# An attention and FFN kernel on Trainium2: narrower waits on the last x1 stores, a gate product two tiles later, two clears on another engine

## What is computed

```python
W = weights[condition]                                  # a style matrix (32x32) per sequence
h = einsum('bct,bcd->bdt', x, W)
q, k, v = split(clip(h @ w_qkv.T, -8, 8))
q, k = layer_norm(q), layer_norm(k)                     # with weight and bias
probs = softmax(causal(q @ k.T * scale + alibi))        # 32 heads of 16
x1 = x + (probs @ v) @ w_out.T

y = einsum('bsi,boi->bso', x1, weight[adapter_ids])     # one of 8 adapters (512x512) per sequence
logits = y @ gate_w
r = sum(top_k(logits, 2))                               # the sum of the two largest
shared = relu(y @ up_w)**2 @ down_w
routed = ((y @ fc1_w @ expert_w) * r) @ fc2_w
out = x1 + layer_norm(shared + routed)
```

## Time and profile before

| what | us |
|---|---|
| median of 3 executions | 1146.95 |
| lowest and highest of them | 1144.14, 1147.49 |
| the profiled execution | 1143.86 |
| its span, from first to last instruction | 1142.1 |

### The profile page before, as it was taken

The page is one execution under the profiler, slowest core; times in us unless marked ns, Lnnn a source line. Parts: engine busy times, 40 slices in busy tenths (PEclk is TensorE's granted clock), DMA queues, the critical chain, the costliest instruction groups (busy, mean ns, idle before and its releaser), DMA issues.

```text
span 1142.1 us, 27399 instructions
## 1 busy us (share of the span) xinstructions
PE 1095.8 (96%) x10996; PEld 892.1 (78%) x10996; DVE 682.4 (60%) x1042; ACT 603.0 (53%) x985; POOL 710.2 (62%) x610
## 2 busy tenths in 40 slices
PE   5999999999999999999999699999999999999994
PEld 3778888888888888888877578787878888787883
DVE  5767666666667666666665156565656545554432
ACT  4466767777767677777776233425161524333220
POOL 4366888888888887888766255556455454533342
PEclk9999999999999999999999899999999999999997
DMA  7035555555555556565487724232514223030100
GB/s 273 30 87 179 182 185 183 184 181 189 177 185 180 186 181 208 184 182 190 150 285 269 292 86 127 92 93 75 133 56 120 70 83 102 28 84 28 46 28 37
DMA packets 95277, 160.77 MB, mean 141 GB/s; under 512 B 46385, under 2 KB 47153, under 8 KB 89777
## 3 DMA queue, kind: packets, MB, share of 16 engines
q1 hardware_dynamic: 77504, 114.23, 30.8%
q0 software_dynamic: 12224, 34.10, 9.4%
q10 hardware_dynamic: 5424, 10.71, 2.6%
HBM read 93.97 MB, written 42.47 MB: 119 GB/s over the span
## 4 chain that ended last, share of the span: by engine, by line
PE 91%; DMA 3%; DVE 2%; issue 1%; SPq 1%; ACT 0%; POOL 0%; DVEq 0%; ACTq 0%; POOLq 0%
PE bank L628 22%; PE pair L812 16%; PE bank L788 15%; PE bank L718 10%; PE bank L805 8%; PE bank L668 7%; PE pair L645 3%; PE pair L690 2%; PE bank L676 2%; PE bank L618 2%; PE bank L703 1%; DMA x_rows<-x1t 1%; PE bank L656 1%; PE bank L758 1%; DMA vx<-v_hl 1%
## 5 line engine op out<-in xcount | busy, mean ns | idle before, releaser
L1664 POOL TENSOR_TENSOR w_lo<-w2t,w_hi 128x2048 fp32r<-128x2048 f32 x38 | 175.1, 4608 | 35.8 <-ACT w_hi L972 32.1
L628 PE MATMUL bank<-wqkv_hi,h_hi 128*128 128x512 f32 x384 | 153.6, 400 | 0.1
L1726 POOL TENSOR_TENSOR u_lo<-act,u_hi 128x512 fp32r<-128x512 f32 x64 | 82.7, 1293 | 113.2 <-ACT u_hi L1165 113.0
L628 PE MATMUL bank<-wqkv_hi,h_lo 128*128 128x512 f32 x384 | 149.8, 390 | 0.0
L628 PE MATMUL bank<-wqkv_lo,h_hi 128*128 128x512 f32 x384 | 149.6, 390 | 0.0
L1513 DVE TENSOR_TENSOR act<-act 128x512 f32<-128x512 f32 x59 | 67.0, 1135 | 57.1 <-ACT act L1161 57.1
L812 PE MATMUL pair<-down_hi,u_hi 128*128 128x512 f32 x256 | 100.9, 394 | 0.0
L812 PE MATMUL pair<-down_hi,u_lo 128*128 128x512 f32 x256 | 100.8, 394 | 0.0
L788 PE MATMUL bank<-yT_hi,up_hi 128*128 128x512 f32 x256 | 100.7, 394 | 0.0
L812 PE MATMUL pair<-down_lo,u_hi 128*128 128x512 f32 x256 | 100.3, 392 | 0.0
L788 PE MATMUL bank<-yT_hi,up_lo 128*128 128x512 f32 x256 | 99.8, 390 | 0.0
(11 more groups left out here) (178 smaller groups left out, 2919.2 us busy)
## 6 DMA issues: line engine op xcount, KB each, us to landing
w2t<-in_w SPq DMA_DIRECT2D x38, 1024.0 KB
vx<-v_hl SPq DMA_DIRECT2D x128, 68.0 KB
x_rows<-x1t SPq DMA_DIRECT2D x32, 256.0 KB, 3.7
x1g<-x_rows SPq DMA_DIRECT2D x32, 256.0 KB, 2.9
kx<-k_hl SPq DMA_DIRECT2D x124, 64.0 KB
ffn_high<-w_high SPq DMA_DIRECT2D x20, 256.0 KB, 3.7
ffn_low<-w_low SPq DMA_DIRECT2D x20, 256.0 KB, 3.4
stage<-in_wqkv SPq DMA_DIRECT2D x3, 1024.0 KB, 8.0
```

Of the source, the lines that this page charges most:

```text
L628: m = e.matmul(into, a[:, c, :], b[:, n, c, :], start=(c == 0 and k == 0), stop=(c == KC - 1 and k == 2))
L1664: e.tensor_tensor(w2_lo[:, :, :], w2t[:, :, :], w2_hi[:, :, :].bitcast(F32), ALU.subtract).then_inc(d_wlo, 1)
L1726: e.tensor_tensor(u_lo[n % FC][:, :], act[n % 2][:, :], u_hi[n % FC][:, :].bitcast(F32), ALU.subtract) \
```

## The change

- **x1 stores.** On ScalarE the wait for both a_store semaphores at u chunk 5 becomes a wait for a_store[0] at chunk 6 and one for a_store[1] at chunk 7.
- **y of group 1.** On SP both halves (1 MB each) are loaded after the load of adapter 27 instead of ahead of the store of x1 tile 31. The gate product of group 1 goes from behind the up chunks of group 0 to behind the down products of its second tile, its transposes and gate_weights(1) to the third tile; the groups after it stay as they are.
- **Adapter 26.** SP loads it after the store of x1 tile 28, no longer ahead of the vx copies of tile 29. The low part of down is fetched in two pieces, seven chunks ahead of w2_hi of slot 26 and one after o_hi of tile 31.
- **Start.** The clears of kx and vx go to GpSimd, as 32-bit words, the first behind the third style product, the second behind v's low part of tile 0. The low half of wo on DVE goes behind v of tile 0. DVE waits for the adapter ids alone, and copies the style ids seven steps later, behind a semaphore of their own.

The diff, cut to its core:

```diff
@@ SP
             for dst, src in ((ids_row[:, :], adapter_ids.broadcast_to([P, BATCHES])),
-                             (ids_col[:, :], adapter_ids.rearrange("o b -> b o")),
-                             (style_col[:, :], style_ids.rearrange("o b -> b o"))):
+                             (ids_col[:, :], adapter_ids.rearrange("o b -> b o"))):
                 e.dma_start(dst, src).then_inc(s_ids, 16)
+            e.dma_start(style_col[:, :], style_ids.rearrange("o b -> b o")).then_inc(s_style, 16)
...
             spread_k(T - 2)
-            load_w2(slot_up(0))
...
             store_x1(T - 4)
+            load_w2(slot_up(0))
             spread_v(T - 1)
...
             store_x1(T - 2)
-            upto(e, "r", T - 1)
-            load_back(1, 0, 0, KC)
-            load_back(1, 1, 0, KC)
             store_x1(T - 1)
...
                 if slot_down(m) < SLOTS:
                     load_w2(slot_down(m))
+                if m == 0:
+                    upto(e, "r", T - 1)
+                    load_back(1, 0, 0, KC)
+                    load_back(1, 1, 0, KC)
@@ TensorE
-                    e.wait_ge(m_down, 32)
+                    e.wait_ge(m_down, 48)
...
-                if ahead:
+                if ahead and m:
                     gate_products(m + 1)
...
                     down(m, t)
-                    if ahead and t == 0:
+                    if m == 0 and t == 1:
+                        gate_products(1)
+                    if ahead and t == (0 if m else 2):
                         turn_gates(m + 1)
@@ ScalarE
             fetch(m_route, route_lo[:, :, :], 1, UP_CHUNKS, ROUTE_CHUNKS)
+            upto(e, "o", T - 1)
+            upto(e, "x1", T - 2)
+            fetch(m_down, down_lo[:, 0:FC - 1, :], 1, UP_CHUNKS + ROUTE_CHUNKS, FC - 1)
             high_w2(slot_up(0))
...
-            upto(e, "x1", T - 2)
-            fetch(m_down, down_lo[:, :, :], 1, UP_CHUNKS + ROUTE_CHUNKS, FC)
+            upto(e, "ot", T - 1)
+            fetch(m_down, down_lo[:, FC - 1:FC, :], 1, CHUNKS - 1, 1)
...
                     if n == EARLY:
                         upto(e, "x1", T - 1)
-                        for k in range(2):
-                            e.wait_ge(a_store[k], 16 * (T // 2))
+                    elif EARLY < n < FC:
+                        e.wait_ge(a_store[n - EARLY - 1], 16 * (T // 2))
...
-                if ahead:
+                if ahead and m:
                     gates_out(m + 1)
...
+                    if m == 0 and t == 1:
+                        gates_out(1)
@@ DVE
-            e.wait_ge(s_ids, 48)
+            e.wait_ge(s_ids, 32)
...
+            e.wait_ge(s_style, 16)
+            step(e.tensor_copy(stylec[:, :], style_col[:, :]))
             step(e.tensor_scalar(style_of[:, :], spread, 0.0, stylec[:, 0:1], ALU.mult, ALU.add))
...
-            e.memset(kx[:, :, :, :], 0.0).then_inc(A["zero"], 1)
...
-                if i == 0:
-                    finish_start()
@@ GpSimd
+                if i == 0:
+                    e.wait_ge(s_wlo, 3)
+                    e.memset(kx[:, :, :, :].bitcast(F32), 0.0).then_inc(A["zero"], 1)
...
                 low_v(i)
+                if i == 0:
+                    e.wait_ge(s_masks, 16)
+                    e.wait_ge(s_wlo, 4)
+                    e.wait_ge(s_tables, 2)
+                    e.memset(vx_words[:, :], 0.0).then_inc(A["zero"], 1)
```

More of the change, by code:

```diff
@@ L247, in program @@
     xt += [asb(f"xt{i}", [P, DM]) for i in (4, 5)]
-    vx = asb("vx", [P, BPT, 2, HEADS, VD], BF16)
+    vx_words = asb("vx", [P, BPT * HEADS * VD])
+    vx = vx_words[:, :].bitcast(BF16).rearrange("p (b n h v) -> p b n h v", b=BPT, n=2, h=HEADS)
     p_hi = asb("p_hi", [P, HEADS * SEQ], BF16)
@@ L330, in program @@
     route_f = [early_route[:, 0, :], early_route[:, 1, :], total[0], total[1]]
+    s_style = sem("s_style")
     s_cst, s_ids, s_masks, s_qkln = sem("s_cst"), sem("s_ids"), sem("s_masks"), sem("s_qkln")
@@ L1389, in _ @@
             step(e.tensor_copy(idc[:, :], ids_col[:, :]))
-            step(e.tensor_copy(stylec[:, :], style_col[:, :]))
             step(e.scalar_tensor_tensor(keyr[:, :], idr[:, :], float(BATCHES), row, ALU.mult, ALU.add))
@@ L1420, in low_weights @@
                 e.tensor_tensor(dst, stage[n][:, :, :], hi.bitcast(F32), ALU.subtract).then_inc(s_wlo, 1)
-            def finish_start():
-                e.wait_ge(s_masks, 16)
-                e.wait_ge(s_wlo, 4)
-                e.wait_ge(s_tables, 2)
-                e.memset(vx[:, :, :, :, :], 0.0).then_inc(A["zero"], 1)
             low_weights(0)
@@ L1443, in _ @@
             low_weights(2)
-            e.wait_ge(s_wlo, 3)
-            e.memset(kx[:, :, :, :], 0.0).then_inc(A["zero"], 1)
             def stats_of(t, n, b, name):
@@ L1480, in _ @@
                 stats_of(i, 0, qn, "cq")
-                if i == 0:
-                    low_weights(3)
                 if 0 <= i - 5 < CHUNKS:
@@ L1490, in _ @@
                 take_v(i)
+                if i == 0:
+                    low_weights(3)
                 if i >= LAG:
@@ L1586, in _ @@
                                            ALU.mult, ALU.add).then_inc(S["res"], 1)
-                    if t == 0 and m + 1 < GROUPS:
+                    if t == (0 if m else 2) and m + 1 < GROUPS:
                         gate_weights(m + 1)
```

## The result

The changed kernel takes 1139.09 us (median of 7, 1137.31 to 1142.26) beside 1144.37 us for the kernel before (median of 7): a ratio of 0.995 with a 95% interval of 0.9932 to 0.9969. Measured once more, on another chip, it was 1139.22 us (median of 6) and again 0.995 (0.9932 to 0.9968). By the first row of runs that is 5.3 us faster, where 13.1 were forecast. The profiled execution is 1138.10 us long, 5.8 under that of before.

The account below looks back on a forecast made before the run. TensorE, 96% busy, was taken as the bound, so only its waits and clock could give. Terms 1.1 + 2.0 + 1.7 + 8.1 + 2.4 - 2.2 = 13.1 us, from 1145.6 to 1132.5 us; range 1128.5 to 1138.5.

Parts of the forecast that it names:

- Part 1: At the start, DVE waits for the adapter ids alone and begins earlier: gain 1.1 us, bounds 0 and 1.2.
- The wait that follows is for gathered rows: At the start, after DVE's earlier tables: weight loads filling the queues could hold the rows, so gain could be 0.
- Part 3: Adapter 26 loaded later, so TensorE no longer waits for tile 29's vx copies: gain 1.7 us, bounds 0 and 1.7.
- a third fetch ... Cost 0: New wait ahead of ScalarE's w_hi of adapter 26 ends about 0.5 us later, still covered by TensorE's work: cost 0.
- Part 2: kx and vx clears moved to GpSimd remove TensorE's wait at the first transposes: gain 2.0 us, bounds 1.0 and 2.0.
- The rival that I named for being slower: Late w2t holds w_hi of adapter 26 and the last output projection: 1150 us or more, chance 0.04.
- Part 4: Later x1 store waits cut the 8.7 us wait at slot 26's adapter product to 0.6: gain 8.1 us, bounds 7.5, 8.7.
- The clock: With only 0.6 us idle before it, slot 26's product runs at 2.4 GHz: gain 2.4 us, bounds 0 and 2.4.
- Part 5: Moving the gate product exposes a TensorE wait for GpSimd's w_lo of adapter 27: cost 2.2 us, bounds 0 and 3.5.
- adapter 27 comes late: Its load shares queues with y's 2 MB, so its product starts 1.8 us later: 1134.3 us, chance 0.06.
- the clock falls again: The new 2.2 us idle brings the low clock, so adapter 27's product costs 5.34 us: 1134.9 us, chance 0.09.
- the wait only moves: u chunk 7 waits for tile 31's x1 store, giving back the handover gain: 1143 us, chance 0.06.

Follow-up runs that it names:

- the run with one wait for DVE: The changed kernel plus a DVE wait for style_bd of tile 1 before the low part of weight 2: 1136.65 us, 0.9917.
- the run of the clears alone: The kernel before with only the kx and vx clears moved to GpSimd and wo's low half behind v of tile 0: 1142.87 us, 0.9981.
- down at old place: The changed kernel with down's low part fetched in one piece at its old place, behind u chunk 3: 1136.27 us, 0.9927.
- early gathers: The changed kernel with GpSimd issuing tile 1's style and x gathers ahead of its style product of tile 0: 1136.92 us, 0.9921.
- adapter 26 at old place: The changed kernel with adapter 26's load put back ahead of the last kx and vx copies: 1137.69 us, 0.9919.
- the run of the store waits: The kernel before with only the x1 store waits moved from u chunk 5 to chunks 6 and 7: 1138.08 us, 0.9946.
- the three mends: The changed kernel with DVE waiting for tile 1's style product, down_lo whole at its old place, adapter 27's low part first: 1131.24 us, 0.989.

## Why the prediction was right or wrong

The direction was right, the size was not: 5.3 us for 13.1, and 1139.1 lies 0.6 us above the range. The steps that failed are the end of part 1 ("The wait that follows is for gathered rows", with 0 as the lowest gain) and the end of part 3 ("a third fetch ... Cost 0"). The base was taken 1.2 us too high (1145.6; the kernel before measured 1144.4); with the right one the forecast would have been 1131.3, further off.

**Part 1, failed.** "Gain 1.1 us. The wait that follows is for gathered rows." The step up to the tables was right (DVE at 5.69). The next step asked only for the landing of the rows, and had 0 as a bound for it. It didn't ask what else GpSimd and DVE do at that moment. GpSimd's gathers and style products got ahead or behind DVE's subtractions by a shift of 0.3 us, and each that falls behind costs 1.8 to 1.9 us. Bound 0 wasn't low enough; the run with one wait for DVE recovered 1.7 us, so the cause is shown. Those 1.7 us are counted from 40.96, the best of the five starts of the changed kernel; from the other four it is 3.0 to 4.3.

**Part 2, right in size at its place, undone by part 1.** 2.0 forecast, 2.4 in the run of the clears alone. The clears cost 1.82 and 1.92 us on GpSimd, for 2.1 estimated. Together with part 1 the start gave 0.4 us in one profile of the changed kernel and lost 2.3 in the other. Behind the late style product the clock fell too, in four of five profiles, in a place where the prediction's rivals had no fall.

**Part 3, right in the gain by one profile, failed in the cover.** The vx wait went (1.8 us between the two milestones, 1.7 forecast). Its size before was one draw: in five profiles with adapter 26 at its old place it was 1.7, 0.8, 0.8, nothing and 2.3 us. And "a third fetch ... Cost 0" was wrong, and so was "ends about 0.5 us later than today". The prediction has no price for the issue of this fetch beyond that half microsecond; at the old place down_lo's took 0.37 us. In the new one it took 2.82, and route_lo's, ahead of it, went from 1.10 to 3.23. Cost in this profile 2.8 us of wait and some 1.6 of clock; in the five other profiles with this order 0.5 to 1.8 us of wait and no clock. The rival that I named for being slower had the very instruction, w_hi of adapter 26, and the very time, 626 us; it looked for the danger in the landing of w2t and not in the list of ScalarE ahead of it.

**Part 4, right.** The wait for xgT_lo went from 8.7 to 0.66 (0.6 forecast), and the part alone gave a ratio of 0.9946. The sub-step "the stores protect only chunks 6 and 7" cost no wait at chunk 7.

**The clock, right at its place.** 1.00 over the product of slot 26, which takes 2.9 us again.

**Part 5, right, and incomplete.** Wait for w_lo 2.0 us for 2.2. That GpSimd's order makes it is shown by the run in which w_lo comes first. The prediction treated the later y as neutral. With y ahead w2t of adapter 27 came 4.4 us late, but not by the sharing of queues of the rival "adapter 27 comes late": the late store of tile 31 held SP's list.

**The rival "the clock falls again"** I gave 0.09. Behind the 2.0 us idle at slot 27 the clock of 655 to 667 us was 1.00 in four profiles (changed, down at old place, early gathers, adapter 26 at old place) and 0.86 in two. The row in this fence is of the changed kernel measured again:

```profile
663.94 0.63 PE L721 MATMUL bank<-w_hi,xgT_hi 128*128 128x512 f32 x1
```

With the wait of 2.66 us in the run of the store waits it is three falls of seven, so 0.09 was too low. From slot 27 to the end of the span the two took 1.6 us more than the changed kernel's first profile, where 2.4 were reckoned. That one idle of 2.0 us in the profile of before had left the clock at 1.00 was one draw, and I took it for a rule.

**The rival "the wait only moves"** fell: no wait at chunk 7 in any profile, the store of tile 31 landed 5.7 us after its issue.

**The sum of it.** 7.3 us short in the first profile: 2.7 at the start, 4.3 around the last output projection, 0.3 of small terms. In the second it is 10.3 short: 5.4 at the start, 0.9 ahead of the values product (a wait of 1.3 us at a scores product put down to "issue", not explained), 2.4 around the last output projection and 1.8 behind slot 27, where the clock fell, less 0.1 of small terms. So the start is the larger miss in most executions. That the first profile looked as if the output projection were, was chance.

## What to carry to other kernels

When an edit moves one engine's list by a few tenths of a microsecond, look at which long VectorE instructions with two SBUF inputs then start just ahead of GpSimd's short ones: each such case cost GpSimd the rest of that instruction here, and a wait put on VectorE can be free. A DMA issue is an instruction of the engine that makes it, and its price grew here with what was under way; price it by the rows at full queues, and keep it out of the list between a value that TensorE waits for and the engine that makes it. An idle near 2 us or above was here a chance of a lower clock, so one profile at the full clock behind it doesn't show that it is safe.

## What the runs showed of the hardware

GpSimd waited for whole instructions of VectorE: a gather issue of 0.94 us took 2.82 and a 128x128 product of 0.46 us took 2.29 when a 2.29 us subtraction of VectorE had started 0.3 us ahead, and neither was longer when it had started first. VectorE's subtraction kept its 2.29 us beside a gather issue that had started first, and took 2.45 beside a style product that had (23.30 and 23.15 in the run of the store waits); so the turns aren't shown to be equal. The Trainium skill ("SBUF — State Buffer", "SBUF: two separate sides") states this rule of the first starter; by it the 2.27 us of DVE alone put 1.98 us ahead of style_bd, and the row has 1.83 more than alone.

ScalarE's DMA issue took from 0.37 to 3.23 us for the same kind of transfer. At 615 to 629 us the DMA share of the changed kernel is full (1.05 of the 16 engines in the window, 383 GB/s). In all 13 profiles the length of route_lo's issue follows the landing of up_lo, issued 10 to 11 us ahead of it on the same queue. Where up_lo landed 0.65 us or more ahead of route_lo's issue (two profiles), it took 0.5 us. Where it landed 0.1 to 0.2 ahead (five, the kernel before among them), it took 1.0 to 1.1. Where it landed 0.6 to 0.8 behind its start (four), it took 1.3 to 1.7, at 1.6 behind (the changed kernel again) 2.3, and at 3.3 behind (the changed kernel) 3.2. An issue that waits for room behind older transfers fits all of this; what the limit is counted in, the runs don't tell.

TensorE's clock behind an idle: 3.3 to 3.4 us brought a fall in four of five profiles at the start. 2.8 us brought one at the last output projection (0.72), 2.7 us one at slot 27 in the run of the store waits (0.83) and 2.3 us one at the values product in the run with adapter 26 at its old place (0.79), while 2.6 us at the start of the three mends left it at 1.00. 2.0 us brought one in two of six at slot 27 and none at 41 us in the kernel before. 1.2 to 1.8 us at the last output projection brought none in four, and 0.7 us none at slot 26 in ten.
